# Norm to top eight of row tiles inside the graph blocks, and the third expert layer in rounds of two tiles with two weight buffers

## The reference, cut to what matters

```python
for L in range(4):
    x = x + gnn_L(layernorm(x), adj)
    x = x + ffn_L(layernorm(x))
# gnn_0: softmax over 1024 keys, one head, 128 columns, plus x @ Wfx     gnn_1: GAT, 4 heads of 64
# gnn_2: (adj==1) @ (V @ w1) + (adj==2) @ (V @ w2) + (adj==3) @ (V @ w3) + bias
# gnn_3: softmax of e and of -e, each @ inp, @ wtrans, elu
# ffn_L: logits = xn @ gate_w (+ gate_b); top 2 of E experts per row; weighed sum of act(xn @ W1[e] + b1[e]) @ W2[e] + b2[e]
#   E = 16, 8, 8, 16; hidden 512, 512, 1024, 512; relu, gelu, gelu, silu; ffn_2 has one more, shared expert for all rows
```

## Time and profile before

| what | value |
|---|---|
| median of three runs | 1241.56 us (1239.06 to 1244.21) |
| the profiled execution | 1240.28 us, of which the span is 1238.2 |
| TensorE busy | 981.2 us (79%) |
| VectorE busy | 738.7 us (60%) |
| ScalarE busy | 513.4 us (41%) |
| GpSimd busy | 456.6 us (37%) |
| DMA | 148.42 MB, mean 120 GB/s |

### The profile page before, as it was taken

How to read it: one execution, slowest core, us unless ns; L and a number is a source line. 1 busy time by engine, 2 the same in 40 slices (tenths; PEclk the granted TensorE clock), 3 DMA queues, 4 the chain that set the end, 5 groups by cost and what they waited for, 6 DMA issues and landing times. The chain is left out here.

```text
span 1238.2 us, 24351 instructions
## 1 busy us (share of the span) xinstructions
PE 981.2 (79%) x7766; PEld 910.4 (74%) x7766; DVE 738.7 (60%) x1715; ACT 513.4 (41%) x943; POOL 456.6 (37%) x572
## 2 busy tenths in 40 slices
PE   5785888437888869748985999999738996699993
PEld 1674877425877759747985999999734885699993
DVE  3666655575788556557334666666454675566664
ACT  2241655300566337513011777777403451244441
POOL 1131554212789227510001455555303440254441
PEclk9697999768899979979986999999958997799997
DMA  6002965400000156632214575553030001547763
GB/s 221 1 2 70 335 225 156 139 12 1 1 1 2 36 175 196 199 112 60 86 35 182 199 290 165 200 187 114 23 127 0 2 1 35 224 167 229 257 211 119
DMA packets 65853, 148.42 MB, mean 120 GB/s; under 512 B 10704, under 2 KB 42736, under 8 KB 59760
## 3 DMA queue, kind: packets, MB, share of 16 engines
q1 hardware_dynamic: 55792, 120.17, 27.9%
q0 software_dynamic: 9984, 27.28, 7.3%
HBM read 203.88 MB, written 18.87 MB: 180 GB/s over the span
## 5 line engine op out<-in xcount | busy, mean ns | idle before, releaser
L1394 PE MATMUL r_pH<-e_xsT,e_w 128*128 128x128 f32 x2624 | 321.4, 281 | 24.5 <-DMA e_w<-w_in 21.9
L1394 PEld LDWEIGHTS r_pH<-e_xsT,e_w 128*128 128x128 f32 x2624 | 309.9, 196 | 29.8 <-issue 16.8
L1342 POOL DMA_INDIRECT y_rows<-e_ys,e_to x104 | 188.9, 1816 | 268.0 <-DVE e_idx L1462 137.0
L1430 ACT ACTIVATE e_w_hi<-e_w 128x1024 fp32r<-128x1024 f32 (+1 forms) x104 | 136.2, 1310 | 118.6 <-DMA e_w<-w_in 117.3
L1407 PE MATMUL r_pY<-e_w_hi,e_h_hi 128*128 128x256 f32 x544 | 164.2, 302 | 9.1 <-issue 4.5
L1474 DVE TENSOR_TENSOR e_w_lo<-e_w,e_w_hi 128x1024 fp32r<-128x1024 f32 (+1 forms) x104 | 160.6, 1544 | 17.5 <-ACT e_w_hi L1430 15.9
L1479 DVE TENSOR_TENSOR e_h_lo<-xnT,e_h_hi 128x512 fp32r<-128x512 f32 (+1 forms) x104 | 88.9, 855 | 129.8 <-ACT e_h_hi L1446 129.6
L1407 PE MATMUL r_pY<-e_w_hi,e_h_lo 128*128 128x256 f32 x544 | 155.5, 286 | 0.0
L1407 PE MATMUL r_pY<-e_w_lo,e_h_hi 128*128 128x256 f32 x544 | 155.3, 286 | 0.0
L352 PE MATMUL g_o<-g_V,g_pT 128*128 128x65 f32 (+2 forms) x896 | 138.7, 309 | 14.8 <-ACT g_pT L312 14.8
L1442 ACT ACTIVATE xnT<-r_pH,e_w 128x128 f32<-128x128 f32 x432 | 119.4, 376 | 73.4 <-PE r_pH L1394 73.3
(11 more groups left out here) (258 smaller groups left out, 1444.0 us busy)
## 6 DMA issues: line engine op xcount, KB each, us to landing
e_w<-w_in SPq DMA_DIRECT2D x60, 1024.0 KB
e_w<-w_in SPq DMA_DIRECT2D x72, 512.0 KB
e_w<-w_in SPq DMA_DIRECT2D x32, 1028.0 KB
e_w<-w_in SPq DMA_DIRECT2D x44, 514.0 KB
e_b<-b_in SPq DMA_DIRECT2D x76, 128.0 KB
e_w<-y_rows SPq DMA_DIRECT2D x24, 256.0 KB, 5.3
p_adj<-adj_in SPq DMA_DIRECT2D x8, 512.0 KB, 7.5
xn_rows<-xn SPq DMA_DIRECT2D x4, 1024.0 KB, 4.4
```

What stands on the lines that cost most here:

```text
L1342: pool.indirect_dma_start(out=y_rows[:, :], in_=ys[b][:, :], in_offset=None, out_offset=bass.IndirectOffsetOnAxis(ap=to[b][:, :], axis=0))\
L1394: ins = nc.tensor.matmul(pH[b % 2][:, f, :], w1[b][:, at:at + P], xsT[b % 2][:, c, :], start=(c == 0), stop=(c == DC - 1))
L1430: nc.scalar.activation(w2_hi[b % 2][:, :], w2[b][:, :], ACT.Copy).then_inc(w2_rounded, 1)
```

## The change

Norm, transposes, logits and top eight of a row tile are put into a class Front with one method per step and tile. In graph0, graph1 and graph3 a new function attend hangs these methods into the unit loop of attention; in graph2 they stand in the tile loops. moments of a tile comes right behind the end of its last unit, norm one unit later, the transposes on TensorE two units later, ScalarE's copy three, logits four and rank five. The unit at whose end tile t is complete is done(t): t + 4 in graph0, 4t + 7 in graph1, 2t + 7 in graph3. In graph0 free is 8: transposes start at unit 8, since their accumulators are those of the scores. Steps that would fall beyond the last unit come behind the loop. Logits of tile t wait until the copy of tile t-1's logits is done (ranked). GpSimd inverts one column at a time. SyncE stores the normed rows tile by tile and waits for all eight stores at the end of the graph block. In graph0 two of the four kinds of instruction behind the last unit move into the preparation, the others into finish, one tile at a time. The gate keeps only what follows L1074.

In the expert layers UN becomes 2 in the third layer (with two weight buffers; the first eight tiles are four written-out rounds, HEAD) and stays 4 in the others. SyncE's bias fetch of tile t-2 stands ahead of the w1 fetch of tile t in all layers that have one. In the third layer results are scattered at t-4 (UN + 2), where UN + 1 would be t-3. combine uses the w1 and w2 buffers together.

```diff
-UN = 4
+UN_NARROW, UN_WIDE = 4, 2
...
+        class Front:
...
+            def store(self, sp):
+                for t in range(NT):
+                    sp.wait_ge(self.xn_ready, t + 1)
+                    sp.dma_start(xn_rows[t * P:(t + 1) * P, :], xn[:, t, 0:D]).then_inc(self.stored, 16)
+                sp.wait_ge(self.stored, 16 * NT)
+
+            def moments(self, dve, t):
+                nc.vector.bn_stats(out=stats[:, t, :], in_=x[:, t, :]).then_inc(self.linked, 1)
+                dve.wait_ge(self.linked, t + 1)
+                nc.vector.bn_aggr(out=mean_var[:, t, :], in_=stats[:, t, :]).then_inc(self.var_ready, 1)
+
+            def invert(self, pool, t):
+                pool.wait_ge(self.var_ready, t + 1)
+                nc.gpsimd.tensor_scalar(mean_var[:, t, 1:2], mean_var[:, t, 1:2], EPS, None, ALU.add)\
+                    .then_inc(self.raised, 1)
+                pool.wait_ge(self.raised, t + 1)
+                nc.gpsimd.tensor_tensor(rstd[:, t, :], mean_var[:, t, 1:2], power[:, t, :], ALU.pow)\
+                    .then_inc(self.rstd_ready, 1)
+
+            def norm(self, dve, t):
+                dve.wait_ge(self.rstd_ready, t + 1)
+                nc.vector.tensor_scalar(xn[:, t, 0:D], x[:, t, :], mean_var[:, t, 0:1], rstd[:, t, :],
+                                        ALU.subtract, ALU.mult).then_inc(self.xn_ready, 1)
+
+            def turn(self, pe, t):
+                n = len(self.tp)
+                pe.wait_ge(self.xn_ready, t + 1)
+                if t >= n:
+                    pe.wait_ge(self.xnT_ready, t - n + 1)
...
+            def place(self, act, t):
+                act.wait_ge(self.turned, t + 1)
+                nc.scalar.activation(xnT[:, :, t * P:(t + 1) * P], self.tp[t % len(self.tp)], ACT.Copy)\
+                    .then_inc(self.xnT_ready, 1)
+
+            def logits(self, pe, t):
+                if t == 0:
+                    pe.wait_ge(self.loaded, self.ALL)
+                else:
+                    pe.wait_ge(self.ranked, t)
+                pe.wait_ge(self.xnT_ready, t + 1)
...
+            def rank(self, dve, link, t):
+                dve.wait_ge(self.summed, t + 1)
...
+                ins.then_inc(self.ranked, 1)
+                dve.wait_ge(self.ranked, t + 1)
+                link(nc.vector.max(out=v8[:, t, :], in_=lg[:, t, 0:self.E]))
+                nc.vector.max_index(out=i8[:, t, :], in_max=v8[:, t, :], in_values=lg[:, t, 0:self.E])
...
+        def attend(block, ph, front, heads, slope, lowest, rows, s, sa, values, width, finish, scores, done, free=0,
+                   settle=None, more=()):
...
+            def turn_at(t):
+                return max(done(t) + 2, free)
+
+            def place_at(t):
+                return max(done(t) + 3, free + 1)
+
+            def logits_at(t):
+                return max(done(t) + 4, free + 2)
+
+            def rank_at(t):
+                return logits_at(t) + 1
...
+            def vector_step(u, dve, link, finished):
+                if "vector_step" in more:
+                    more["vector_step"](u, dve, link, finished)
+                for t in range(NT):
+                    if done(t) + 1 == u:
+                        front.norm(dve, t)
+                    if done(t) == u:
+                        measure(dve, finished, t)
+                    if rank_at(t) == u:
+                        front.rank(dve, link, t)
...
+                        dve.wait_ge(copied, 4)
+                        link(nc.vector.tensor_tensor(f01[:, 1, :], f01[:, 1, :], f01[:, 0, :], ALU.subtract))
+                        nc.vector.tensor_tensor(x[:, :, OUT:D], x[:, :, OUT:D], bc(f01[:, 0:1, :], [P, NT, OUT]), ALU.add)
                         for t in range(4, NT):
                             mask_of(t)
...
+                def finish(u, dve, link, o, gm):
+                    nc.vector.tensor_scalar(has[:, u:u + 1], gm, MASKED / 2, None, ALU.is_gt)
                     link(nc.vector.reciprocal(r[:, u:u + 1], o[:, OUT:OUT + 1]))
+                    link(nc.vector.scalar_tensor_tensor(
+                        out=x[:, u, OUT:D], in0=f01[:, 1, :], scalar=has[:, u:u + 1], in1=x[:, u, OUT:D],
+                        op0=ALU.mult, op1=ALU.add))
...
                         ins.then_inc(summed, 1)
+                        if t >= 3:
+                            front.logits(pe, t - 3)
+                        if t >= 2:
+                            front.turn(pe, t - 2)
...
                         nc.vector.tensor_tensor(x[:, t, :], x[:, t, :], pso[t % 2][:, :], ALU.add).then_inc(added, 1)
+                        if t >= 1:
+                            front.norm(dve, t - 1)
+                        dve.wait_ge(added, t + 1)
+                        front.moments(dve, t)
+                        if t >= 4:
+                            front.rank(dve, link, t - 4)
+                    front.norm(dve, NT - 1)
+                    for t in range(NT - 4, NT):
+                        front.rank(dve, link, t)
...
+            UN = un = UN_WIDE if shared else UN_NARROW
+            T = loop_tiles(E, first, UN)
...
+            HEAD = max(2, first // UN)
+            LAG = UN + (2 if shared else 1)
...
+                        if b2_name and not early(i, b, 2):
+                            bias(*before(i, b, 2))
                         e = sp.value_load(etab[0:1, bass.ds(t, 1)], min_val=0, max_val=EN - 1)
...
-                        if b2_name and not early(i, b, 2):
-                            bias(*before(i, b, 2))
...
-                        if not early(i, b, UN + 1):
-                            store(*before(i, b, UN + 1), y_stored[(b - 1) % UN])
-                    gate_rstds(pool)
+                        if not early(i, b, LAG):
+                            store(*before(i, b, LAG), y_stored[(b - LAG) % UN])
                     pool.wait_ge(rows_known, 1)
-                    pool.wait_ge(rows_stored, 16)
                     last = loop(pool, step)
-                    store(last - 1, UN - 1, y_stored[UN - 1])
+                    for b in range(2 * UN - LAG, UN):
+                        store(last - 1, b, y_stored[b])
```

More of the change, by code:

```diff
@@ L75, in build @@
         pair_row = keep("pair_row", [P, 2, NT])
+        lg = keep("lg", [P, NT, 16])
+        v8 = keep("v8", [P, NT, 8])
+        i8 = keep("i8", [P, NT, 8], U32)
         sems = []
@@ L728, in _ @@
                             .then_inc(adjT_loaded[t % 2], 16)
-                    sp.wait_ge(masked, NT)
+                        if t == 1:
+                            front.load(sp)
+                    front.store(sp)
                 @block.tensor
@@ L757, in _ @@
                         ins.then_inc(summed, 1)
+                        if t >= 3:
+                            front.logits(pe, t - 3)
+                        if t >= 2:
+                            front.turn(pe, t - 2)
+                    for t in range(NT - 2, NT):
+                        front.logits(pe, t - 1)
+                        front.turn(pe, t)
+                    front.logits(pe, NT - 1)
                 @block.gpsimd
@@ L761, in _ @@
                     norm_gpsimd(pool, var_ready, rstd_ready)
+                    for t in range(NT):
+                        front.invert(pool, t)
                 @block.scalar
@@ L768, in _ @@
                         nc.scalar.activation(high[:, t, :, :], first12[t % 2][:, :, :], ACT.Copy).then_inc(rounded, 1)
+                    for t in range(NT):
+                        front.place(act, t)
                 @block.vector
```

316 lines of the change are left out of this document (183 added, 133 removed).

## The result

| kernel | median us | runs | ratio to before |
|---|---|---|---|
| before | 1241.64 (1237.88 to 1247.35) | 8 | 1 |
| changed | 1229.45 (1220.67 to 1235.60) | 8 | 0.9913 [0.9887, 0.9939] |

A forecast was written before the change was run, and what follows sets the result against it. Limits read by stage: serial seams, TensorE in graph blocks 3 and 4 and the third expert layer, interleaved chains in block 2. 1240.3 - 40.9 (seams) + 23.4 (blocks) - 10.3 (third layer) - 2.0 (bias): 1210 us, range 1202 to 1220.

The forecast's parts named there:

- Graph block 2 ... I take 4.0, ... between 0 and 11: Second graph block: front steps added to its unit loop cost 4.0 us, between 0 and 11.
- A: GpSimd's turn: power costs 1.68 us on one column too, at seams and in graph block 2; 1228 us, chance 0.14.
- B: Third expert layer: two buffers don't cover the fetch, 19 us of stalls instead of 3; 1226 us, chance 0.10.
- If nothing is swallowed: Graph block 2: the worse of two interleaved chains pays 7 tiles x 1.0 = 7.0 us.
- rival E: Graph blocks 1, 2, 4: GpSimd's six pushed into mask and shift, slope 2.4 us late per tile; 1255 us, chance 0.03.
- The seams: Four seams between graph blocks and expert layers: 27.0 us together instead of 67.9, giving back 40.9.
- The relay of ranks: At the seams, with several tiles outstanding, logits wait for the last copy: about 0.75 us for each tile.
- 0.6 more for four ranks that start on a TensorE just stopped: Seam 4: an estimated 0.6 us extra within its 6.4 us.
- Graph block 4: Fourth graph block: TensorE's turns and logits 2.7 us, 1.0 for what doesn't fit; 3.7, between 2.7 and 8.
- 1.6 us ... four times: Graph block 3: TensorE idles 1.6 us at logits awaiting a rank, tiles 4 to 7; 6.4 of its 9.8 us.
- 3 us, between 0 and 10: Third expert layer: stalls on weight fetches with two buffers, against 13.3 us saved by two fewer tiles.
- the bias order: Bias fetch ahead of w1: 2.0 us gained at the end of the first expert layer, nothing elsewhere.

The follow-up runs named there:

- b1: Changed kernel with graph block 2's whole front behind the unit loop, ranks left behind blocks 1, 2 and 4 done in one go: ratio 0.9905 to before.
- b4: Changed kernel with eight small bf16 products, results thrown away, ahead of each unit's transposes in graph block 2: ratio 0.9874 to the kernel before.
- c2: Changed kernel with small products in graph block 2, block 3 logits one tile later (transposes first behind its loop), and batched remaining ranks: 1210.42 us, ratio 0.9764 to before.
- c4: Changed kernel with block 2's small products, its logits and ranks behind the unit loop, ranks batched behind blocks 1, 2, 4: 1226.39 us, one profiled execution.
- c1: Changed kernel with eight small products per unit and GpSimd's addition and power done twice per tile in graph block 2: 1249.10 us, one profiled execution.
- a3: Changed kernel with transposes, copy, logits and rank one unit sooner in graph block 2: ratio 0.9903 to the kernel before.
- d2: Changed kernel with GpSimd's pair behind the next unit's six small instructions in graph block 2, norm to rank one unit later: ratio 0.9908 to before.
- a2: Changed kernel with GpSimd's addition and power done by ScalarE as ln and exp in graph block 2: ratio 1.0030 to the kernel before.
- b3: Changed kernel with logits behind the loops not waiting for the previous rank, and one rank for all that are left: ratio 0.9928 to before.
- b2: Changed kernel with logits of graph block 3 one tile later: ratio 0.9856 to the kernel before.
- a4: Changed kernel with rounds of four and four weight buffers in the third expert layer: ratio 1.0045 to the kernel before.
- c3: Changed kernel with the bias fetch back behind the fetch of w2: ratio 0.9954 to the kernel before.
- d1: Changed kernel with block 2's small products, later block 3 logits, batched remaining ranks, and GpSimd's pair one unit later in block 2: ratio 0.9787 to before.

## Why the prediction was wrong

**The step that failed is "Graph block 2 ... I take 4.0, ... between 0 and 11".** It measured 16.5. Put into the sum, this alone moves it from 1210 to 1223, beyond the forecast's 1202 to 1220. The measured 1229.45 does lie inside the wide range of 1196 to 1231, and close to rivals A (1228) and B (1226), but by luck: neither mechanism happened (the power takes 0.57 us undisturbed, the waits for weights are 2.3 us). The 16.5 has two parts.
- *The clock, some 8.8 us.* The prediction priced every delay of a unit as time, and none as a pause of TensorE. It read the third expert layer and the blocks 3 and 4 as TensorE's, block 2 as one with waits to spare, and there idle time of TensorE seemed free. It isn't: three tiles pay 2.8 us each, 8.4, for a clock at half for 6.8 us each time. b1 (no front, no falls behind the first tile) and b4 (front and dummy products, no falls) show cause and price.
- *At full clock, some 7.7 us* (block 2 in c2, 161.3, less 153.5): 1.0 to 1.1 in each whole tile but the first, where 4.0 over seven tiles is 0.6. That is inside the bounds of 0 to 11, and near the 7.0 that the prediction had for "If nothing is swallowed". What pays for it is only in part known. Logits and ranks hardly do (c4), as the prediction said of VectorE's waits. Moments and norm, 1.0 us of VectorE on the chain, were in the loop in every run but b1, and so were TensorE's transposes and ScalarE's copy; no run takes one of them out alone. The other candidate is GpSimd. The row had said that it has no rest, and the text used it for rival E and not for the sum. A second pair costs 1.7 us at clock 1.00 (c1), and neither time beside the moments (a3) nor another place in the queue (d2), where the pair takes 0.8 us instead of 2.6, wins anything back. That speaks for the amount of GpSimd's work and against its place, but it is argued, not shown: no run has less of that work with nothing in its stead (a2 put table loads there), and one tile of c1 is all that stands at clock 1.00.

**The seams** came to 33.2 us and not 27.0. The relay of ranks was the term: forecast 0.75 a step, measured 1.3 in seam 1. Here are logits of that seam from TensorE's timeline, and its last 9.5 us as a stretch:

```profile
92.32 0.62 PE L227 MATMUL g_S<-g_front_gw,xnT 128*128 128x16 f32 x4 [0.82 <-DVE lg L236]
93.20 0.86 PE L227 MATMUL g_S<-g_front_gw,xnT 128*128 128x16 f32 x4 [0.27 <-DVE lg L236]
...
98.51 1.01 PE L227 MATMUL g_S<-g_front_gw,xnT 128*128 128x16 f32 x4
...
99.82 1.00 PE L227 MATMUL g_S<-g_front_gw,xnT 128*128 128x16 f32 x4
```

```profile
93.70:103.20 9.50, 6.84 (x30) 5.74 (x30) 4.74 (x28) 1.53 (x4) 0.79 (x2) 0.50 0.08 28
```

Most of the difference is the clock again. The one step at clock 1.00, from 92.32 to 93.20, takes 0.88 us. Behind it the clock is 0.50, TensorE's four instructions take 1.0 us where the row of before has 0.52 at clock 1.00, and a step takes 1.3. By these rows (an estimate) four steps at half clock are 1.7 of the 2.5 us that seam 1 is over, and three in seam 4 are its whole 1.3. The smaller part, 0.88 against 0.75, fits a second slip: the copy waits for the end of the four instructions, not for the 0.37 to the next start that the prediction read in a full queue. "0.6 more for four ranks that start on a TensorE just stopped", put on seam 4 alone, was the only term near this and belonged to every seam. The mean clocks of the four seams are 0.56, 0.64, 0.60 and 0.65, where before they were 0.90, 0.87, 0.70 and 0.76. The 56 products of ones stood ahead of the transposes then; what they would give back in a seam of today no run shows. Batched ranks take back 1.6 and 0.8 (b3).

**Graph block 4** paid 6.9 and not 3.7. Its tiles are 9.5 us apart instead of 8.8, at clock 1.00, but for two of 10.0 and 10.3. The 0.7 is about the 0.62 of TensorE's new work for each tile; the sum had it for five turns and four logits only, and gave 1.0 to all the rest. No run takes the block apart further.

**What held.** Graph block 3: the wait of logits for a rank, "1.6 us ... four times", was there four times with 1.45 us (a tile with it takes 8.07, in b2 6.36), and moving the logits by one tile removed it. The sum, 10.7 for 9.8, is near by some luck: the fourth wait fell into the seam, and a fall of the clock in one tile, 1.5 us, took its place. Graph block 1: 6.2 against 5.9, which tests little, since its 4.9 isn't the sum of the terms named (four units at 1.3 are 5.2 already). Seam 2: 5.8 against 5.5. The third expert layer: 30 rises, 2.3 us of waits for weights and 3.1 us of longer distances against "3 us, between 0 and 10". It came out 3.1 better than the sum in the profile (13.4 against 10.3), of which 2.2 lie behind the last rise, while a4 gives 8.5 to 9.7, so no more can be made of that difference. No run varies the store and gather orders. For the bias order 2.0 us were booked; c3 doesn't show them.

**The rivals.** A (the power costs 1.68 on one column too) was wrong as told: 0.57 undisturbed, over the 0.35 taken. But beside the mask and the shift it takes 1.47 us in most tiles of b4, near the full price, for rival E's reason. E named the mechanism, GpSimd's six pushed into mask and shift and the slope late for it, and set 2.4 us for each of 24 tiles and a chance of 0.03. Its price came in block 2 only, where the slope waits 3.04 us for the six; there all of the front cost 1.0 us a tile at full clock, and the clock added what made 2.4 the right size by chance (16.5 over 7 tiles is 2.4). The Trainium skill (SBUF — State Buffer, Who interferes with whom) says that a VectorE instruction with two SBUF inputs holds up a GpSimd instruction that reads SBUF. The trace agrees: 128x1 instructions on GpSimd go from 0.2 to 1.1 or 1.2 us where they meet L338 or L346, and the power from 0.57 to 1.47. That page also bears on what the prediction made of it, that moments and norm, with one input, would do GpSimd no harm. The trace agrees here too (L381 and L382 take 0.19 us beside the moments at 389.66), but it wasn't the point: the pair itself runs beside mask and shift, and the six behind it come late.

## What to carry to other kernels

When work is put into a loop, look at the helper engine on the way as well: here GpSimd is busy for 12.4 of 13.4 us a tile, much of it held up by VectorE, and a second pair on it cost 1.7 us. Read TensorE's waits for where they lie and not for their sum alone, since waits that move closer together can halve its clock for microseconds, and a few products that compute nothing may be the cheapest cure. For the same reason look at what such products do before they are taken out, and at the granted clock of the row that a price is read from: logits that took 0.52 us at 1.00 took 1.0 at 0.50. In a chain of single tiles count the time until a result can be read, not the distance of starts in a full queue.

## What the runs showed of the hardware

- TensorE's granted clock fell to 0.50 for 6.8 us behind 3 us with 1.32 us of work, in a stretch where it is busy for about 80% of the time; the longest wait in it was 1.12 us. Behind another 3 us with 1.37 us of work it stayed at 1.00. Before, with waits up to 1.1 us too but more evenly spread, it stayed at 1.00 over six tiles. A tile at 0.80 on the mean took 17.2 us, one at 1.00 14.4.
- Eight bf16 products of 128x128 for each unit, some 32 more instructions a tile, held the clock at 1.00 in all tiles of b4, c2 and d1 behind the first, for 0.1 us a tile at most. In c4 one tile stood at 0.89 all the same, and with GpSimd's pair doubled the eight were not enough (0.82 and 0.90).
- Four fp32 logits of 128x16 took 0.52 us at clock 1.00 and 1.0 at 0.50, and a step of the relay between TensorE and VectorE 0.88 and 1.3.
- On ScalarE ln and exp in turn loaded a table each time, 1.28 us apiece, 16 loads in graph block 2.
- GpSimd's power on a 128x1 column takes 0.57 us, against 1.68 on eight columns.
